# TensorE's order in a scan step: both rough score products ahead of the step's sums

## The chip, the cores and the metric

The kernel runs on one core of a Trainium2 chip. The metric is the device time of one launch in microseconds. The median of three runs of the kernel before is 12530.81 us (12523.07 to 12570.84). Engines are named as in the profile: PE is TensorE, DVE is VectorE, ACT is ScalarE, POOL is GpSimd, SP is SyncE, which issues most of the transfers.

## The reference

For each of 16 images of 192 channels and 32 x 32 positions, four layers run one after the other, each on the group-normalised input and added to it:

```
x = x + attention(gn(x))      # 6 heads of 32, softmax over 1024 positions
x = x + selective_scan(gn(x)) # 4 directions, 192 channels, 16 states, 1024 steps
x = x + top_k_mask(gn(x))     # depthwise conv, 30 largest of each channel kept
x = x + chunked_scan(gn(x))   # Mamba-2 block with 12 heads, chunks of 128
```

The second layer's recurrence, for every direction k, channel d and state n, is

```
h = h * exp(dt * A) + (dt * u) * b      # along 1024 positions
y = sum over n of h * c
```

Its dt is softplus of a projection with a bias. The first layer's softmax needs the largest score of each row, and the kernel takes it from a rough bf16 product.

## The kernel before

One loop runs over the images. In its first part two things are woven together: the **scan** of image b (second layer) and the **front** of image b+1, which is that image's attention, its norms and the set-up of its own scan (projections, dt and its softplus).

The scan has 96 steps (`NSTEP`), each with 128 rows (16 channels x 8 states) of 1024 positions. Step i is made of:
- POOL, L1234: the input dt*u*b of step i+3, into one of ten buffers;
- ACT, L1127 (`decay`): exp(dt*A) into the one PSUM tile `ps[2]`. The decay of step i+1 is written in step i and waits until scan i has read the tile;
- DVE, L1189: the scan itself. In every fourth step (`from_psum`, i % 4 == 1) the scan leaves its result in PSUM (L1179) and DVE multiplies by c itself (L1186); in the other steps POOL multiplies (L1250);
- PE, L1015 (`sums`): the sum over states of step i-2, four matmul records in the trace.

The front is written as 192 **half slots** (`HS`), two to a step. Each engine has a generator for it (`front_pe`, `front_act`, `front_dve`, `front_pool`, `front_sp`), and the scan's function of that engine calls `next(front)` twice in a step: on ACT, DVE and POOL once before and once after the step's own main instruction. So an item of an even half slot stands ahead of the step's decay (ACT) or scan (DVE), an item of an odd one behind it. Engines run their instructions in this written order; semaphores couple them. The tables at L516 to L525 give each item its half slot. Those that matter here:
- `PROJECT`, `VALUES` (steps 4 to 19, all in even half slots): the q, k and v projections, PE L675 and L687.
- `ROUGH` (half slots 17 to 112, one product in each): the rough product, PE L700, into the one PSUM bank `bank(3)`. In the next half slot DVE takes its row maximum (L917), and the next product waits for that.
- `UNIT`: 16 attention units for each of three pairs of heads. A unit is the scores (PE L725), their exp (ACT L869, one half slot later for the first two pairs, in the same one for the third) and, together with the next unit's scores, the sums of the weighted values (PE L737). I call the pairs 0, 1 and 2. Pair 0 has even half slots (52 to 82), pair 1 odd ones (87 to 117), pair 2 both.
- `MAX_ROWS`: the maxima turned into a row, PE L711, once DVE has joined them (L921), then copied by ACT (L832).
- `OUT_AT`: output projection (PE L749), added by DVE (L902) two half slots later; then the norm (`norm_*`), the transposed copy (ACT L880) and `LOWERED` (PE L760, ACT L885).
- `DT_AT`: six dt projections, PE L772 (`steps_of`). Two half slots later ACT adds the bias (L890), three later DVE clamps (L940), four later ACT takes the exp (L894).

On PE the step is written as

```
next(front)          # even half slot
if i >= 2:
    sums(i - 2)
next(front)          # odd half slot
```

Of the kernel before, what the change touches and what calls it, by code (L numbers as in the profile page):

```python
# [88 lines left out]
def build(nc, x, out, wqk, wv, wp, pb, xpw, dtw, dtb, alog, ds, lnw, lnb, cw, cb, wz, wx, wdt,  # L89
# [3 lines left out]
    with ctx:  # L93
# [424 lines left out]
        ROUGH = [17, 49, 81]  # L518
        MAX_ROWS = [49, 84, 119]
        UNIT = [[52 + 2 * k for k in range(16)], [87 + 2 * k for k in range(16)], [122 + 4 * k // 3 for k in range(16)]]  # L520

        EXP_LAG = (1, 1, 0)
        OUT_AT = (156, 158, 160, 162)
        LOWERED = (171, 172, 174, 175)
        DT_AT = (176, 178, 180, 182, 184, 186)  # L525

# [56 lines left out]
        def front_sp(sp, image):  # L583
            for hs in range(HS):
                t, m = sums_at(hs - 1)
                if t is not None:
                    sp.wait_ge(a_oc, 2 * t + m + 1)
                    for e in range(2):
                        rows, c = rows_of_head(2 * t + e)
                        sp.dma_start(OA[rows, c, HALF * m:HALF * m + HALF], OC[64 * e:64 * e + DH, :]).then_inc(a_u, 16)  # L590
                if hs == 165:
                    sp.wait_ge(a_x, 4)
                    for c, m in enumerate(CT):
                        sp.dma_start(x1_d[image, 128 * c:128 * c + m, :], XI[0:m, c, :]).then_inc(f_x, 16)
                if hs == 171:
                    sp.wait_ge(g_xn, 4)
                    for c, m in enumerate(CT):
                        sp.dma_start(xn_d[image, 128 * c:128 * c + m, :], XN[0:m, c, :]).then_inc(f_n, 16)
                for s in range(2):
                    if hs == 175 + 3 * s:  # L600
                        sp.wait_ge(m_xc, 2 * s + 2)
                        sp.dma_start(bc_d[image, s, :, :], XD[0:RP, s, :]).then_inc(m_bw, 16)
                yield
# [46 lines left out]
        def front_pool(pool):  # L650
            for hs in range(HS):
# [5 lines left out]
                if m == 1 and t >= 1:  # L657

                    c, n = t - 1, CT[t - 1]
                    pool.wait_ge(a_u, 64 * (t + 1))  # L660
                    pool.wait_ge(a_rl, 32 * (t + 1))
                    pool.tensor_tensor(OA[0:n, c, :], OA[0:n, c, :], RDB[0:n, c, :], ALU.mult).then_inc(a_o, 1)
                if hs == 169:
                    norm_pool(pool, 1)
                yield

        def front_pe(pe):
# [108 lines left out]
            for hs in range(HS):  # L776
# [18 lines left out]
                if hs in OUT_AT:  # L795
                    project_out(OUT_AT.index(hs) // 2, OUT_AT.index(hs) % 2)
                if hs == 167:
                    norm_pe(pe, 1)
# [7 lines left out]
        def front_act(act, stored):  # L806
            for hs in range(HS):
# [55 lines left out]
                if t is not None:  # L863
# [3 lines left out]
                    for e in range(2):  # L867
                        act.wait_ge(a_st, 2 * u + e + 1)
                        nc.scalar.activation(PT[:, 2 * (u % 2) + e, :], bank(e), ACT.Exp,  # L869
                                             scale=DH ** -0.5).then_inc(a_e, 1)  # L870
                if hs == 166:
                    norm_square(act, 1)
                if hs == 170:
                    norm_act(act, 1, (128, 128))
                if hs in (171, 172):

                    c = hs - 171
                    act.wait_ge(g_xn, 4)
# [18 lines left out]
        def front_dve(dve, image):  # L897
# [7 lines left out]
            for hs in range(HS):  # L905
# [20 lines left out]
                if hs - 2 in OUT_AT:  # L926
                    add(OUT_AT.index(hs - 2) // 2, OUT_AT.index(hs - 2) % 2)
                if hs == 161:
                    dve.wait_ge(a_x, 2)
                    norm_stats(0, XI)  # L930
                if hs == 165:
                    dve.wait_ge(a_x, 4)
                    norm_sums(dve, 1, XI, begun=True)
                if hs == 168:
                    norm_var(dve, 1)
# [71 lines left out]
        def scan_pe(pe, front):  # L1007
# [13 lines left out]
            for i in range(NSTEP):  # L1021
                next(front)
                if i >= 2:
                    sums(i - 2)
                next(front)

# [50 lines left out]
        def scan_sp(sp, b, front):  # L1077
            for i in range(NSTEP):
# [15 lines left out]
                if i % 2 == 0:  # L1094
# [3 lines left out]
                    if i + 2 * DTR < NSTEP:  # L1098
                        sp.wait_ge(m_da, i + 2)
                        spread_dt(sp, b, i + 2 * DTR, m_dtl[i // 2 % DTR])  # L1100
                if i == 93:

# [916 lines left out]
```

## Time and profile before

| | before |
|---|---|
| median of three runs | 12530.81 us |
| the profiled execution's own time | 12556.06 us |
| its span, first to last instruction | 12554.3 us |
| granted TensorE clock, mean | 0.839 |
| PE busy | 9985.9 us (80%) |
| DVE busy | 8321.4 us (66%) |
| POOL busy | 7736.3 us (62%) |
| ACT busy | 4365.6 us (35%) |
| L1186 on DVE, 384 times | mean 1225 ns |
| L869 on ACT, 1632 times | mean 591 ns |
| L921 on DVE, 51 times | mean 3649 ns |

Span and run time differ by under 2 us. No engine is busy all the time: the engines wait for each other in turn, and the engine with the largest share is not for that reason the bound. The granted clock is the share of TensorE's full 2.4 GHz that the chip gave; it is 1.0 or 0.5 at any moment, so 0.839 is a mix. Matmul records overlap in time, so their starts say more than their durations.

### The profile page before, as it was taken

The page shows a single profiled execution, that of the slowest core. Times are in us where ns is not written, and L with a number is a line of the kernel's source. Part 1 is how long each engine was busy: PE and PEld are TensorE (multiplying, and loading weights), DVE is VectorE, ACT ScalarE, POOL GpSimd, SP SyncE. Part 2 cuts the span into 40 slices and gives each one's busy share as a digit, 9 for nine tenths or more (in the row PEclk, how much of TensorE's full clock was granted, in tenths as well). Part 3 has the DMA queues.
Part 4 walks back from the last instruction along what each step waited for, and adds up shares of the span by engine and source line. Part 5 has one row for each costly group of instructions (what it writes and reads, how often), then busy time and mean ns, then how long its engine had stood idle before and what let it go on. Part 6 is the DMA issues. An engine that isn't in the chain of part 4 may idle for free. (4 is left out here: it accounts for less than half of the span.)

```text
span 12554.3 us, 91878 instructions
## 1 busy us (share of the span) xinstructions
PE 9985.9 (80%) x28440; PEld 2877.6 (23%) x28440; DVE 8321.4 (66%) x7943; ACT 4365.6 (35%) x5374; POOL 7736.3 (62%) x3710
## 2 busy tenths in 40 slices
PE   6787877878778787878878778787878878778787
PEld 1112222122222212122122222212122122222212
DVE  2367666667666667666667666667666767667666
ACT  1243333424334233333423334243333423334243
POOL 0384766837567474766847567484766847567583
PEclk9697878879788787888979788887878979788897
DMA  0352542524335242542524335152543524345252
GB/s 14 90 123 63 125 106 69 123 67 118 86 93 138 49 119 63 122 110 69 123 68 114 88 93 138 49 119 63 125 106 73 124 67 116 83 97 134 56 122 56
DMA packets 358663, 1181.05 MB, mean 94 GB/s; under 512 B 67483, under 2 KB 68747, under 8 KB 358023
## 3 DMA queue, kind: packets, MB, share of 16 engines
q1 hardware_dynamic: 331703, 1157.28, 37.0%
q10 hardware_dynamic: 24800, 15.62, 0.5%
q8 instruction: 259, 4.24, 0.1%
q14 instruction: 381, 3.12, 0.1%
q0 software_dynamic: 1520, 0.78, 0.0%
HBM read 1004.06 MB, written 156.02 MB: 92 GB/s over the span
## 5 line engine op out<-in xcount | busy, mean ns | idle before, releaser
L1234 POOL TENSOR_TENSOR arena<-arena 128x1024 f32<-128x1024 f32 x1536 | 3666.8, 2401 | 734.6 <-issue 712.3
L1250 POOL TENSOR_TENSOR arena<-arena 128x1024 f32<-128x1024 f32 x1152 | 2713.9, 2356 | 1414.1 <-DVE arena L1189 1411.7
L1015 PE MATMUL ps<-arena,sel_y 128*32 128x512 f32 x6144 | 3307.6, 673 | 231.2 <-POOL arena L1250 208.7
L1189 DVE TENSOR_TENSOR_SCAN arena<-ps,arena 128x1024 f32<-128x1024 f32 x1152 | 2630.2, 2283 | 773.4 <-ACT ps L1127 711.9
L1127 ACT ACTIVATE ps<-arena,v_na 128x1024 f32<-128x1024 f32 x1536 | 1716.3, 1117 | 3461.1 <-DVE arena L1189 2214.7
L917 DVE TENSOR_REDUCE arena<-ps 128x1 bf16<-128x512 f32 x1632 | 1115.0, 683 | 1259.2 <-PE ps L700 1259.2
L1015 PEld LDWEIGHTS ps<-arena,sel_y 128*32 128x32 f32 x6144 | 601.3, 118 | 2420.0 <-issue 2046.6
L869 ACT ACTIVATE arena<-ps 128x512 f32<-128x512 f32 x1632 | 879.7, 591 | 774.5 <-PE ps L725 774.1
L725 PE MATMUL ps<-arena 33*128 33x512 f32 x3264 | 988.2, 684 | 111.7 <-ACT arena L869 85.7
L1179 DVE TENSOR_TENSOR_SCAN ps<-ps,arena 128x1024 f32<-128x1024 f32 x384 | 878.0, 2286 | 297.0 <-ACT ps L1127 289.2
L700 PE MATMUL ps<-arena 32*128 32x512 bf16 x1632 | 678.6, 416 | 476.8 <-DVE arena L917 476.0
L737 PE MATMUL ps<-arena 128*64 128x512 f32 x3264 | 993.6, 691 | 0.0
L410 PE MATMUL ps<-g_mv,c_group 128*128 128x3 f32 (+1 forms) x528 | 128.1, 338 | 870.5 <-DVE g_mv L361 540.3
L417 POOL TENSOR_TENSOR g_t<-g_t,v_root 128x2 f32<-128x2 f32 x66 | 46.3, 702 | 973.1 <-DVE g_t L379 973.1
L700 PEld LDWEIGHTS ps<-arena 32*128 32x128 bf16 x1632 | 151.1, 93 | 1680.8 <-DVE arena L917 1076.6
L1186 DVE TENSOR_TENSOR arena<-ps,arena 128x1024 f32<-128x1024 f32 x384 | 470.4, 1225 | 45.8 <-DVE ps L1179 7.5
L1686 DVE SCALAR_TENSOR_TENSOR arena<-arena,v_mcw 128x1024 f32<-128x1024 f32 (+1 forms) x384 | 456.9, 1190 | 13.1
L1696 POOL TENSOR_SCALAR arena<-arena,v_mcw 128x640 f32<-128x640 f32 x144 | 164.2, 1143 | 463.6 <-ACT arena L1594 463.6
L1668 POOL TENSOR_TENSOR arena<-arena,c_heads 88x1536 bf16<-88x1536 bf16 x112 | 313.2, 2797 | 186.0 <-ACT arena L1622 176.9
L1858 POOL TENSOR_TENSOR arena<-arena 128x384 f32<-128x384 f32 x128 | 106.3, 830 | 482.3 <-DVE arena L1760 482.3
L725 PEld LDWEIGHTS ps<-arena 33*128 33x128 f32 x3264 | 258.8, 194 | 529.2 <-issue 273.0
L1594 ACT ACTIVATE arena<-ps 128x1024 f32<-128x1024 f32 x64 | 65.8, 1028 | 878.1 <-PE ps L1439 878.1
(217 smaller groups left out, 12005.8 us busy)
## 6 DMA issues: line engine op xcount, KB each, us to landing
arena<-scan_dtu SPq DMA_DIRECT2D x770, 512.0 KB, 6.1
arena<-scan_dt SPq DMA_DIRECT2D x770, 512.0 KB, 4.7
arena<-scan_bc SPq DMA_DIRECT2D x260, 512.0 KB, 6.9
scan_dt<-arena SPq DMA_DIRECT2D x68, 512.0 KB, 8.1
scan_dtu<-arena SPq DMA_DIRECT2D x68, 512.0 KB, 4.8
scan_dt<-arena SPq DMA_DIRECT2D x68, 256.0 KB, 4.1
scan_dtu<-arena SPq DMA_DIRECT2D x68, 256.0 KB, 4.7
XN<-arena SPq DMA_DIRECT2D x204, 64.0 KB, 4.3
```

The source lines that it names most:

```text
L700: nc.tensor.matmul(bank(3), QR[at:at + DH, t, Q * j:Q * j + Q], KR[at:at + DH, t, HALF * m:HALF * m + HALF], start=True, stop=True).then_i ...
L725: nc.tensor.matmul(bank(e), KK[r, t, Q * j:Q * j + Q], QQ[r, t, HALF * m:HALF * m + HALF], start=True, stop=True).then_inc(a_st, 1)
L737: mm = nc.tensor.matmul(bank(2)[64 * e:64 * e + 64, :], V[:, j, 2 * t + e, :], PT[:, 2 * (u % 2) + e, :], start=(j == 0), stop=(j == 7))
L869: nc.scalar.activation(PT[:, 2 * (u % 2) + e, :], bank(e), ACT.Exp, scale=DH ** -0.5).then_inc(a_e, 1)
L917: nc.vector.reduce_max(MXH[:, i // 2, i % 2:i % 2 + 1], bank(3), AX.X).then_inc(a_m, 1)
L1015: mm = nc.tensor.matmul(ps[3][32 * q:32 * q + 32, HALF * h:HALF * h + HALF], sel_y[:, r, :], step[:, i % NBUF, HALF * h:HALF * h + HALF], ...
L1127: nc.scalar.activation(ps[2][:], dtr[:, i // 2 % DTR, :], ACT.Exp, scale=v_na[:, at:at + 1]).then_inc(m_da, 1)
L1179: nc.vector.tensor_tensor_scan(ps[2][:, o], ps[2][:, o], step[:, i % NBUF, o], 0.0, ALU.mult, ALU.add).then_inc(m_h, 1)
L1186: nc.vector.tensor_tensor(step[:, i % NBUF, :], ps[2][:], Cb[2 * (k // 2) + f], ALU.mult).then_inc(m_hcv, 1)
L1189: nc.vector.tensor_tensor_scan(step[:, i % NBUF, o], ps[2][:, o], step[:, i % NBUF, o], 0.0, ALU.mult, ALU.add).then_inc(m_h, 1)
L1234: pool.tensor_tensor(step[:, i % NBUF, :], dur[:, i // 2 % DUR, :], Bb[2 * (k // 2) + f], ALU.mult).then_inc(m_bu, 1)
L1250: pool.tensor_tensor(step[:, i % NBUF, :], step[:, i % NBUF, :], Cb[2 * (k // 2) + f], ALU.mult).then_inc(m_hcp, 1)
```

## The change

On PE `sums(i - 2)` moves behind the second half slot. Every table entry from pair 1 on is raised by one half slot, and so are the fixed half slots of the norm, the copies and the transfers. The first `MAX_ROWS`, pair 0, `PROJECT`, `VALUES` and `ROUGH` keep theirs.

```diff
-        MAX_ROWS = [49, 84, 119]
-        UNIT = [[52 + 2 * k for k in range(16)], [87 + 2 * k for k in range(16)], [122 + 4 * k // 3 for k in range(16)]]
+        MAX_ROWS = [49, 85, 120]
+        UNIT = [[52 + 2 * k for k in range(16)], [88 + 2 * k for k in range(16)], [123 + 4 * k // 3 for k in range(16)]]
...
-        OUT_AT = (156, 158, 160, 162)
-        LOWERED = (171, 172, 174, 175)
-        DT_AT = (176, 178, 180, 182, 184, 186)
+        OUT_AT = (157, 159, 161, 163)
+        LOWERED = (172, 173, 175, 176)
+        DT_AT = (177, 179, 181, 183, 185, 187)
...
             for i in range(NSTEP):
                 next(front)
+                next(front)
                 if i >= 2:
                     sums(i - 2)
-                next(front)
```

The rest of the diff adds one to `hs == 165, 171, 175 + 3 * s` (SP), `169` (POOL), `167` (PE), `166, 170, 171, 172` (ACT), `161, 165, 168` (DVE), and turns SP's `i == 93` into `i == 94`. The order of SP's queue comes out the same.

PE in the steps with projections (about steps 9 to 15). L675 is a projection, L700 a rough product, L1015 the sums. Before:

```order
L700 MATMUL ps<-arena 128x512
L675 MATMUL ps<-XN,w_q 128x512 x2
L700 MATMUL ps<-arena 128x512
L1015 MATMUL ps<-arena,sel_y 32x512 x2
L700 MATMUL ps<-arena 128x512
```

After:

```order
L675 MATMUL ps<-XN,w_q 128x512 x2
L700 MATMUL ps<-arena 128x512 x2
L1015 MATMUL ps<-arena,sel_y 32x512 x2
L675 MATMUL ps<-XN,w_k 128x512 x2
L700 MATMUL ps<-arena 128x512 x2
```

The sums stood between the step's two rough products; now the two stand side by side, and sums and projection follow each other.

PE in the steps of pair 0 (steps 27 to 41). L725 are the scores, L737 the weighted values. Before:

```order
L700 MATMUL ps<-arena 128x512 x2
L725 MATMUL ps<-arena 128x512 x2
L737 MATMUL ps<-arena 64x512 x2
L1015 MATMUL ps<-arena,sel_y 32x512 x2
L700 MATMUL ps<-arena 128x512 x2
```

After:

```order
L700 MATMUL ps<-arena 128x512
L725 MATMUL ps<-arena 128x512 x2
L737 MATMUL ps<-arena 64x512 x2
L700 MATMUL ps<-arena 128x512
L1015 MATMUL ps<-arena,sel_y 32x512 x2
L700 MATMUL ps<-arena 128x512
```

The odd product stood behind unit and sums, right before the next even one. Now it stands between unit and sums.

ACT in the last steps (89 to 95). L1127 is the decay of the scan's next step, L890 the bias of a dt projection, L894 the exp of the one before. Before:

```order
L890 ACTIVATE arena<-ps,v_dtb 128x1024
L1127 ACTIVATE ps<-arena,v_na 128x1024
L894 ACTIVATE arena<-arena 128x1024
L890 ACTIVATE arena<-ps,v_dtb 128x1024
L1127 ACTIVATE ps<-arena,v_na 128x1024
L894 ACTIVATE arena<-arena 128x1024
L634 ACT_TABLE_LOAD
```

After:

```order
L890 ACTIVATE arena<-ps,v_dtb 128x1024
L1127 ACTIVATE ps<-arena,v_na 128x1024
L894 ACTIVATE arena<-arena 128x1024
L890 ACTIVATE arena<-ps,v_dtb 128x1024
L894 ACTIVATE arena<-arena 128x1024
L634 ACT_TABLE_LOAD
```

These are the last rows of the scan; the pattern of the first three repeats before them. All L890 and L894 have moved behind one decay more: the last decay stood behind the last L890, and now the last L890 stands behind the last decay. On DVE the clamps (L940) stay where they were, each right before a scan.

## Rows read from the trace of the kernel before

**Rows 1.** Waits: engine and line, waited for: us in total, times, longest us.
```profile
DVE arena L917 <- PE ps L700: 1259.2, 811, 24.2
```
**Rows 2.** Timeline, PE and DVE, one step of pair 0, third image: start, us, instruction [idle before <-releaser].
```profile
2239.41 2.28 DVE L1189 TENSOR_TENSOR_SCAN arena<-ps,arena 128x1024 f32<-128x1024 f32 x1
...
2239.56 0.39 PE L700 MATMUL ps<-arena 32*128 32x512 bf16 x1 [0.79 <-DVE arena L917]
...
2241.61 0.67 DVE L917 TENSOR_REDUCE arena<-ps 128x1 bf16<-128x512 f32 x1
...
2241.95 1.90 PE L1015 MATMUL ps<-arena,sel_y 128*32 128x512 f32 x4
...
2243.79 0.40 PE L700 MATMUL ps<-arena 32*128 32x512 bf16 x1
...
2244.22 0.69 DVE L917 TENSOR_REDUCE arena<-ps 128x1 bf16<-128x512 f32 x1 [1.94 <-PE ps L700]
...
2244.97 0.40 PE L700 MATMUL ps<-arena 32*128 32x512 bf16 x1 [0.79 <-DVE arena L917]
```
**Rows 3.** Windows, steps 26 to 41, 16 images: stretch, length, busy by engine, clock.
```profile
5921.96:6024.27 102.31, 88.22 (x219) 18.31 (x220) 63.64 (x55) 34.57 (x48) 67.00 (x29) 0.83 0.42 97
...
sum 1574.98, PE 1354.34 PEld 283.39 DVE 1018.41 ACT 552.52 POOL 1061.73; mean PE 84.65 PEld 17.71 DVE 63.65 ACT 34.53 POOL 66.36
```
**Rows 4.** The same over steps 43 to 56, pair 1; one image, and the sum.
```profile
759.58:825.23 65.65, 61.79 (x188) 14.10 (x187) 53.56 (x48) 32.78 (x45) 58.37 (x25) 1.00 0.65 153
...
sum 1050.04, PE 988.26 PEld 225.16 DVE 856.89 ACT 524.30 POOL 934.23; mean PE 61.77 PEld 14.07 DVE 53.56 ACT 32.77 POOL 58.39
```
**Rows 5.** Timeline, PE, one step with a projection, third image.
```profile
2082.12 0.39 PE L700 MATMUL ps<-arena 32*128 32x512 bf16 x1
...
2082.45 2.18 PE L675 MATMUL ps<-XN,w_k 128*128 128x512 f32 x4
...
2084.56 0.40 PE L700 MATMUL ps<-arena 32*128 32x512 bf16 x1
...
2084.88 1.90 PE L1015 MATMUL ps<-arena,sel_y 128*32 128x512 f32 x4
...
2086.72 0.40 PE L700 MATMUL ps<-arena 32*128 32x512 bf16 x1
```
**Rows 6.** Windows, steps 20 to 25 of the first image.
```profile
629.50:660.72 31.22, 23.91 (x55) 4.65 (x53) 25.12 (x22) 8.13 (x8) 27.79 (x13) 0.73 0.52 119
```
**Rows 7.** Windows over steps 9 to 19 of 16 images, the sum.
```profile
sum 897.78, PE 866.15 PEld 250.09 DVE 663.23 ACT 289.30 POOL 743.85; mean PE 54.13 PEld 15.63 DVE 41.45 ACT 18.08 POOL 46.49
```
**Rows 8.** Timeline, ACT and DVE, steps 90 to 95, third image.
```profile
2496.14 2.28 DVE L1189 TENSOR_TENSOR_SCAN arena<-ps,arena 128x1024 f32<-128x1024 f32 x1
...
2502.89 1.11 ACT L890 ACTIVATE arena<-ps,v_dtb 128x1024 f32<-128x1024 f32 x1 [0.22 <-PE ps L772]
...
2503.91 1.11 ACT L1127 ACTIVATE ps<-arena,v_na 128x1024 f32<-128x1024 f32 x1
...
2504.04 1.28 DVE L940 TENSOR_SCALAR arena<-ps,v_dtb 128x1024 f32<-128x1024 f32 x1 [0.26 <-ACT arena L890]
...
2505.24 2.28 DVE L1189 TENSOR_TENSOR_SCAN arena<-ps,arena 128x1024 f32<-128x1024 f32 x1
...
2512.70 1.12 ACT L1127 ACTIVATE ps<-arena,v_na 128x1024 f32<-128x1024 f32 x1 [1.20 <-DVE arena L1186]
...
2513.83 1.06 ACT L894 ACTIVATE arena<-arena 128x1024 f32<-128x1024 f32 x1
...
2513.92 2.29 DVE L1189 TENSOR_TENSOR_SCAN arena<-ps,arena 128x1024 f32<-128x1024 f32 x1
...
2514.79 1.10 ACT L890 ACTIVATE arena<-ps,v_dtb 128x1024 f32<-128x1024 f32 x1
...
2516.30 1.12 ACT L1127 ACTIVATE ps<-arena,v_na 128x1024 f32<-128x1024 f32 x1 [0.41 <-DVE arena L1189]
...
2517.52 2.29 DVE L1189 TENSOR_TENSOR_SCAN arena<-ps,arena 128x1024 f32<-128x1024 f32 x1
```

More of the change, by code:

```diff
@@ L590, in front_sp @@
                         sp.dma_start(OA[rows, c, HALF * m:HALF * m + HALF], OC[64 * e:64 * e + DH, :]).then_inc(a_u, 16)
-                if hs == 165:
+                if hs == 166:
                     sp.wait_ge(a_x, 4)
@@ L594, in front_sp @@
                         sp.dma_start(x1_d[image, 128 * c:128 * c + m, :], XI[0:m, c, :]).then_inc(f_x, 16)
-                if hs == 171:
+                if hs == 172:
                     sp.wait_ge(g_xn, 4)
@@ L599, in front_sp @@
                 for s in range(2):
-                    if hs == 175 + 3 * s:
+                    if hs == 176 + 3 * s:
                         sp.wait_ge(m_xc, 2 * s + 2)
@@ L662, in front_pool @@
                     pool.tensor_tensor(OA[0:n, c, :], OA[0:n, c, :], RDB[0:n, c, :], ALU.mult).then_inc(a_o, 1)
-                if hs == 169:
+                if hs == 170:
                     norm_pool(pool, 1)
@@ L796, in front_pe @@
                     project_out(OUT_AT.index(hs) // 2, OUT_AT.index(hs) % 2)
-                if hs == 167:
+                if hs == 168:
                     norm_pe(pe, 1)
@@ L870, in front_act @@
                                              scale=DH ** -0.5).then_inc(a_e, 1)
-                if hs == 166:
+                if hs == 167:
                     norm_square(act, 1)
-                if hs == 170:
+                if hs == 171:
                     norm_act(act, 1, (128, 128))
-                if hs in (171, 172):
-                    c = hs - 171
+                if hs in (172, 173):
+                    c = hs - 172
                     act.wait_ge(g_xn, 4)
@@ L927, in front_dve @@
                     add(OUT_AT.index(hs - 2) // 2, OUT_AT.index(hs - 2) % 2)
-                if hs == 161:
+                if hs == 162:
                     dve.wait_ge(a_x, 2)
                     norm_stats(0, XI)
-                if hs == 165:
+                if hs == 166:
                     dve.wait_ge(a_x, 4)
                     norm_sums(dve, 1, XI, begun=True)
-                if hs == 168:
+                if hs == 169:
                     norm_var(dve, 1)
@@ L1100, in scan_sp @@
                         spread_dt(sp, b, i + 2 * DTR, m_dtl[i // 2 % DTR])
-                if i == 93:
+                if i == 94:
                     sp.wait_ge(m_dtp, 6)
```

## The prediction

> **What bounds the kernel now.** I read the waits first, then the timeline of one step in each stage, then the same stage over all 16 images with the windows. The waits say that DVE idles 1259 us for the rough products [rows 1]: that is the wait the change is aimed at. The timeline shows how it arises in a step of pair 0 [rows 2]. PE starts an even product at 2239.56, then unit and sums (2241.95), and only then the odd product (2243.79): 4.23 us. DVE had finished the maximum it depends on at 2242.28 (2241.61 + 0.67) and then sits idle 1.94 us. From the odd product over its maximum (2244.22, 0.69 us) to the next even product (2244.97) it is 1.18 us, in which PE has 0.33 us of work. So a step lasts 5.41 us: PE's row of work, plus a wait of 0.85 us in which PE has nothing it may start.
>
> Over the 16 images the 16 steps of this stage take 1574.98 us, 98.4 an image or 6.15 a step [rows 3]. That is 0.74 us a step more than 5.41. The granted clock there lies below 1, down to 0.83 in the image shown, so part of the time TensorE runs at 1.2 GHz and not at 2.4. In the stage of pair 1, where the unit stands between the odd and the even product, the same work takes 1050.04 us over 16 images and 14 steps: 4.69 a step, at a clock of 1.00 [rows 4].
>
> In the steps with projections [rows 5] the same happens as with pair 1: even product to odd 2.16 us (sums between them), odd to even 2.44 us (projection between them). Both gaps are longer than the 1.18 us of the maximum, which is thereby hidden.
>
> **The change, part by part (for one image, times 16 at the end).**
>
> *Pair 0, steps 26 to 41.* The order becomes even product, unit, odd product, sums. Even to odd is 2.39 us of PE work (2239.56 to 2241.95), odd to even 0.33 + 1.84 = 2.17; both exceed 1.18, so a step is 4.56 us, PE's own work. DVE's round is shorter: scan to maximum 2.20, maximum 0.67, next product after 0.06, its result after 0.43, maximum to scan 0.61, together 3.97. DVE's own product, 1.2 us in every fourth step (L1186 in the profile's table), lifts that step to about 5.2. This is the pattern of pair 1, so I take its measured 4.69 a step, 75.0 us for 16 steps against 98.4: -23.4. The bounds of what is left of the half clock are 0 (as with pair 1) and 11.8 (16 x 0.74, all of it). I take 3, since the stage before this one runs at a lowered clock, 0.73 in the image shown [rows 6]: **-20.4 us**.
>
> *Projections and values, steps 9 to 19.* Here the change undoes what the order had. It becomes projection, even product, odd product, sums. Even to odd is now the naked 1.18, then 0.33 + 1.84 for odd product and sums, then projection and even product at 2.10: 5.45 us a step. DVE does not bound it, not even in its long step (0.43 + 0.61 + 2.20 + 1.2 = 4.4 after the odd product, and the even product's result is there after 4.7). The stage has 11 steps, 60.0 us, against 897.78 / 16 = 56.1 [rows 7]: +3.9. To that comes the clock. PE was busy 54.1 of 56.1 us here; now 0.85 us of each 5.45 are a wait with nothing to do, as in pair 0 before, 0.85 of 5.41. There it cost 0.74 us a step [rows 2, 3]. The bounds are 0 and 11 x 0.74 = 8.1; I take 6.5, because the two rounds are nearly alike: **+10.4 us**.
>
> *Weighed against the Trainium skill.* "TensorE: Matmul & The Clock Gate" (HAM oscillation, and the table at its end) says that TensorE stays warm as long as there are no long idle gaps between bursts of matmuls. The rows of pair 0 speak against it: no gap there is longer than 1.2 us, and the clock is still 0.83. By that rule the clock would add nothing to the projections; this is the first rival below.
>
> *The first row of maxima, step 24.* It stays in half slot 49, and the sums now wait behind it and behind DVE's long L921. Before step 25's first product PE then has 1.84 us of sums left, at half clock 3.7. DVE's own scan and product cover part of it. Bounds 0 and 2.6, I take **+1.3**. Between 20 and 26, where PE has only products and sums, the DVE round of 3.97 rules as before: 0.
>
> *The biases and clamps of dt, steps 90 to 95.* This is the price that the change's table hides. ACT's L890 stood ahead of the decay and ran while DVE scanned; the decay started at the end of the scan or just behind it (2502.89 and 2503.91), and the clamp (2504.04) ran on DVE beside the decay. From scan to scan this was 3.74 us. Moved by one half slot, exp and bias stand behind the decay, which waits for the scan, while DVE still wants the clamp before its next scan. So everything follows in one file: scan to decay 2.38 (2513.92 to 2516.30), decay to exp 1.13 (2512.70 to 2513.83), exp to bias 0.96, bias to clamp 1.15 (2502.89 to 2504.04), clamp to scan 1.20: 6.82 us [rows 8]. From scan 90 to scan 95 there are five such rounds and one such product, 35.3 us, against 2517.52 - 2496.14 = 21.4: +13.9. The first bias, before scan 90, waits for PE today as well; there it can cost 0 to 1.1 (its own duration), I take 0.6: **+14.5 us**. Nothing covers this: PE, POOL and DVE all wait for the next scan, and the set-up behind the scan (its logarithms) starts later by as much.
>
> *What costs nothing.* The exps of pairs 1 and 2 move behind the decay. For pair 1 the scan ends 3.24 us after the odd product (0.43 + 0.61 + 2.20); decay (1.1) and two exps (0.6 each) end at 5.5, and the next scores start only at 2.17 + 0.33 in the next step, at 7.1. For pair 2, PE's row of three units and two sums in two steps stays the same, and the decay has over a microsecond of room. DVE's additions of the output projection move behind the scan; they no longer hold up scan 79, but what ends this stage is PE's row of projections and sums up to the group's end, which is the same, so I count 0, with 0 to -4 as bounds. The norm's steps land in the shadow of a decay. POOL's order and SP's are practically the same.
>
> Sum: -20.4 + 10.4 + 1.3 + 14.5 = **+5.8 us an image, +93 us in all**. The profiled execution's own time is 12556.06; it becomes 12649. It lies 25 us above the median of the runs, and against that median I predict **12624 us**. A difference under 0.5%, 63 us, can't be told from none here; that is 3.9 us an image.
>
> **The rivals.**
>
> *The clock stays full in the projections* (the skill's rule). Then that term is +3.9, the sum -0.7 an image: 12520 us, no change. For it: in these stages the clock was 1 so far. Against it: the idle share will be the one of pair 0. 0.22.
>
> *The clamps do not close the round*, the faster side. The mechanism: if ACT could finish exp and bias before the scan wants its clamp, the last steps would keep 3.74 us. Its place is ACT's queue from step 89 on, its price the 13.9; it decides when a round stays under about 5 us. Then it is -8.1 an image, 12401 us, 1% faster. Against it stands the order itself: L890 is behind L1127, and L1127 waits for the scan. 0.08.
>
> *Pair 0 keeps its half clock* (DVE's own product in every fourth step leaves PE idle about 0.7 us, and a low clock carried over from step 25 may persist). Then pair 0 gives -11.6 only, the sum is +14.6, 12765 us. Against it: pair 1 has the same idle time and never lost its clock. 0.12.
>
> *The change does not do what it says*: the step of pair 0 stays at 5.41, because ACT's exp behind the decay holds the next scores. The sum would be +26, 12950 us. Against it: by the count above the exp ends 1.6 us before the scores need it. 0.03.
>
> **How the numbers follow.** The forecast has 0.55, pair 0's half clock 0.12, the change that fails 0.03: mostly slower. The full clock (0.22) is no change but for little on either side, the open round 0.08 is faster. Of the forecast's own 0.55 I count 0.47 as slower and 0.08 as no change, since its terms together move by 4 us an image. Slower 0.64, same 0.26, faster 0.10. The range takes in the full clock at its lower end and half of the way to pair 0's half clock at its upper: 12510 to 12740.
>
> **What would show it.** Steps of pair 0 at 4.6 us with a clock near 1, and DVE's wait for L700 there gone. Steps 9 to 19 at 5.45 and more, with DVE waiting for L700 and a clock under 1. From 90 to 95 about 6.8 us from scan to scan, with DVE's L940 waiting for ACT's L890. The prediction is wrong if the last steps keep 3.74 us, or if pair 0 gains under 15 us an image.

## The result and the profile after

| | before | changed |
|---|---|---|
| median | 12534.56 us (12523.07 to 12570.84) | 12748.86 us (12724.75 to 12776.83) |
| profiled execution, its own time | 12556.06 us | 12776.83 us |
| its span | 12554.3 us | 12775.0 us |
| granted clock, mean | 0.839 | 0.833 |
| PE busy | 9985.9 us | 10041.8 us |
| L921 on DVE, 51 times, mean | 3649 ns | 4492 ns |

The changed kernel is slower: the ratio is 1.0164, with a 95% interval of 1.0143 to 1.0185. The forecast was 12624 us and its range ended at 12740, so the direction was right and the size was not. It missed by 125 us of 12749.

Spans from decay to decay by stage give the bill. Every number is the mean over 16 images, in us; the stages outside the scan are taken from decay 95 to the next image's decay 0 (15 of them), and "forecast" is the term on record.

| stage | before | changed | difference | forecast |
|---|---|---|---|---|
| steps 0 to 8 | 41.3 | 41.1 | -0.2 | 0 |
| 9 to 19, projections and values | 56.1 | 67.3 | +11.2 | +10.4 |
| 20 to 25, first row of maxima | 31.3 | 33.1 | +1.8 | +1.3 |
| 26 to 41, pair 0 | 98.4 | 85.3 | -13.1 | -20.4 |
| 43 to 56, pair 1 | 65.6 | 67.7 | +2.1 | 0 |
| 62 to 73 | 58.3 | 57.3 | -1.0 | 0 |
| 78 to 89, output projection | 63.5 | 59.3 | -4.2 | 0 (0 to -4) |
| 90 to 94, and outside the scan | 20.9 and 268.8 | 34.1 and 272.5 | +13.2 and +3.7 | +14.5 |

Steps 42, 57 to 61 and 74 to 77 are left out; they differ by -0.1, +0.3 and 0.0. Over the whole span the changed kernel is 220.7 us longer, 13.8 an image, where the forecast had 5.8.

Here are the windows of the changed kernel (columns as in [rows 3]): steps 9 to 19, 26 to 41, 43 to 56 and 90 to 94, each with one image and the sum of 16. They answer to [rows 7], [rows 3] and [rows 4].

```profile
5156.19:5223.04 66.85, 58.96 (x122) 15.57 (x121) 42.39 (x35) 18.41 (x22) 46.72 (x20) 0.87 0.40 94
...
sum 1077.53, PE 951.32 PEld 247.30 DVE 678.28 ACT 295.07 POOL 747.45; mean PE 59.46 PEld 15.46 DVE 42.39 ACT 18.44 POOL 46.72
...
5256.70:5342.54 85.84, 76.13 (x222) 16.86 (x221) 68.64 (x55) 34.54 (x49) 66.09 (x29) 0.96 0.53 124
...
sum 1364.70, PE 1220.94 PEld 270.06 DVE 1084.33 ACT 552.90 POOL 1061.49; mean PE 76.31 PEld 16.88 DVE 67.77 ACT 34.56 POOL 66.34
...
5346.74:5414.37 67.63, 61.87 (x202) 14.46 (x201) 53.84 (x48) 30.95 (x43) 58.38 (x25) 1.00 0.63 148
...
sum 1083.24, PE 990.75 PEld 230.65 DVE 860.94 ACT 494.94 POOL 934.28; mean PE 61.92 PEld 14.42 DVE 53.81 ACT 30.93 POOL 58.39
...
5573.23:5607.14 33.91, 27.09 (x52) 6.41 (x50) 18.63 (x11) 14.53 (x15) 14.88 (x7) 0.85 0.16 45
...
sum 544.85, PE 455.42 PEld 110.26 DVE 298.14 ACT 232.87 POOL 222.69; mean PE 28.46 PEld 6.89 DVE 18.63 ACT 14.55 POOL 13.92
```

In pair 0 two things differ. PE's busy time fell from 84.65 to 76.31 us an image [rows 3]: that is the clock coming back (0.96 in the image shown, 0.95 over the 16, where the kernel before has 0.87). But DVE's busy time rose from 63.65 to 67.77, although its work is the same 55 instructions in the image shown. Something on DVE got longer. In the projections PE is busy 59.46 us instead of 54.13 [rows 7], at a clock of 0.87: the half clock has moved there.

The last steps behave as the prediction drew them. ACT and DVE, third image, answering to [rows 8]: decay, exp and bias stand in a file behind the scan, then the clamp, and from scan to scan it is 2532.76 - 2526.06 = 6.70 us.

```profile
2526.06 2.28 DVE L1189 TENSOR_TENSOR_SCAN arena<-ps,arena 128x1024 f32<-128x1024 f32 x1
...
2528.43 1.12 ACT L1127 ACTIVATE ps<-arena,v_na 128x1024 f32<-128x1024 f32 x1 [3.61 <-DVE arena L1189]
2529.49 1.04 ACT L894 ACTIVATE arena<-arena 128x1024 f32<-128x1024 f32 x1
2530.44 1.09 ACT L890 ACTIVATE arena<-ps,v_dtb 128x1024 f32<-128x1024 f32 x1
...
2531.56 1.28 DVE L940 TENSOR_SCALAR arena<-ps,v_dtb 128x1024 f32<-128x1024 f32 x1 [3.22 <-ACT arena L890]
2532.76 2.28 DVE L1189 TENSOR_TENSOR_SCAN arena<-ps,arena 128x1024 f32<-128x1024 f32 x1
```

Step by step, pair 0 divides cleanly. Most steps have the 4.56 us that the count of PE's work gave (3.98 where there is less on PE, 5.89 with DVE's own product). Two kinds stand out. Steps 34 and 50 take 7.00 and 6.99 us, where they took 5.45 and 4.57. And step 41 takes 10.58 us on average, where it took 7.37. These are DVE's rows of step 34, third image:

```profile
2236.74 0.68 DVE L917 TENSOR_REDUCE arena<-ps 128x1 bf16<-128x512 f32 x1
2239.75 1.28 DVE L1164 SCALAR_TENSOR_TENSOR arena<-arena,v_dsum,ps 128x1024 f32<-128x1024 f32 x1 [2.33 <-PE ps L1015]
2240.95 0.69 DVE L917 TENSOR_REDUCE arena<-ps 128x1 bf16<-128x512 f32 x1
```

L1164 is `taken`, which adds a finished group's sums to the output. On DVE it stands behind the maximum of the even product (2236.74) and ahead of the maximum of the odd one (2240.95), and it waits for the sums of two steps earlier. Those sums now come behind the odd product. So DVE idles 2.33 us, while the odd product's result lies ready behind `taken`, and the next even product waits for its maximum. And these are DVE's and POOL's rows of step 41, third image:

```profile
2272.45 0.67 DVE L917 TENSOR_REDUCE arena<-ps 128x1 bf16<-128x512 f32 x1
2273.15 6.70 DVE L921 TENSOR_TENSOR arena<-arena 128x16 bf16<-128x16 bf16 x1
2279.78 0.68 DVE L917 TENSOR_REDUCE arena<-ps 128x1 bf16<-128x512 f32 x1
...
2270.47 2.37 POOL L1234 TENSOR_TENSOR arena<-arena 128x1024 f32<-128x1024 f32 x1
2272.79 2.37 POOL L1250 TENSOR_TENSOR arena<-arena 128x1024 f32<-128x1024 f32 x1
2275.10 4.72 POOL L1234 TENSOR_TENSOR arena<-arena 128x1024 f32<-128x1024 f32 x2
```

L921 is the maximum of the two halves' row maxima, 16 numbers a lane. It starts while POOL works, and ends at 2279.85, when POOL's third operation in a row ends (2275.10 + 4.72 = 2279.82). In the same step of the kernel before it was held for only one of POOL's operations:

```profile
2253.14 1.91 DVE L921 TENSOR_TENSOR arena<-arena 128x16 bf16<-128x16 bf16 x1
...
2252.66 2.35 POOL L1250 TENSOR_TENSOR arena<-arena 128x1024 f32<-128x1024 f32 x1 [0.80 <-DVE arena L1189]
2254.98 4.74 POOL L1234 TENSOR_TENSOR arena<-arena 128x1024 f32<-128x1024 f32 x2
```

Mean durations of L921 over 16 images are 2.82, 1.91 and 6.87 us in steps 25, 41 and 57 of the kernel before, and 1.91, 5.83 and 6.55 in the changed one. The long form was in the trace of before: in step 57 of every image, and in step 25 of four of them (7.27 to 7.65 us), but never in step 41.

### The profile page after: what moved, and what is told of

It reads as the page before. It is cut to its first block and busy times, and to the rows that moved or that the text cites. A ratio compares the mean times of both kernels' runs of the same rounds, so it can differ in the third digit from the quotient of the medians.

```text
span 12775.0 us, 91878 instructions
## 1 busy us (share of the span) xinstructions
PE 10041.8 (79%) x28440; PEld 2912.4 (23%) x28440; DVE 8380.2 (66%) x7943; ACT 4357.3 (34%) x5374; POOL 7723.9 (60%) x3710
## 5 line engine op out<-in xcount | busy, mean ns | idle before, releaser
L1250 POOL TENSOR_TENSOR arena<-arena 128x1024 f32<-128x1024 f32 x1152 | 2717.4, 2359 | 1624.6 <-DVE arena L1189 1623.1
L1015 PE MATMUL ps<-arena,sel_y 128*32 128x512 f32 x6144 | 3340.5, 690 | 177.5 <-POOL arena L1250 155.0
L1127 ACT ACTIVATE ps<-arena,v_na 128x1024 f32<-128x1024 f32 x1536 | 1717.1, 1118 | 4145.6 <-DVE arena L1189 2604.3
L700 PE MATMUL ps<-arena 32*128 32x512 bf16 x1632 | 683.0, 419 | 528.1 <-DVE arena L917 528.0
L1015 PEld LDWEIGHTS ps<-arena,sel_y 128*32 128x32 f32 x6144 | 607.4, 119 | 2136.3 <-issue 1829.6
L725 PE MATMUL ps<-arena 33*128 33x512 f32 x3264 | 992.9, 687 | 119.0 <-ACT arena L869 114.4
L737 PE MATMUL ps<-arena 128*64 128x512 f32 x3264 | 958.8, 668 | 0.0
L700 PEld LDWEIGHTS ps<-arena 32*128 32x128 bf16 x1632 | 151.1, 93 | 1775.7 <-DVE arena L917 1040.7
L1686 DVE SCALAR_TENSOR_TENSOR arena<-arena,v_mcw 128x1024 f32<-128x1024 f32 (+1 forms) x384 | 456.9, 1190 | 13.1
L725 PEld LDWEIGHTS ps<-arena 33*128 33x128 f32 x3264 | 259.9, 195 | 541.3 <-ACT arena L869 264.0
L940 DVE TENSOR_SCALAR arena<-ps,v_dtb 128x1024 f32<-128x1024 f32 x102 | 131.0, 1284 | 347.7 <-ACT arena L890 347.7
```

The source lines that it names most:

```text
L700: nc.tensor.matmul(bank(3), QR[at:at + DH, t, Q * j:Q * j + Q], KR[at:at + DH, t, HALF * m:HALF * m + HALF], start=True, stop=True).then_i ...
L725: nc.tensor.matmul(bank(e), KK[r, t, Q * j:Q * j + Q], QQ[r, t, HALF * m:HALF * m + HALF], start=True, stop=True).then_inc(a_st, 1)
L737: mm = nc.tensor.matmul(bank(2)[64 * e:64 * e + 64, :], V[:, j, 2 * t + e, :], PT[:, 2 * (u % 2) + e, :], start=(j == 0), stop=(j == 7))
L1015: mm = nc.tensor.matmul(ps[3][32 * q:32 * q + 32, HALF * h:HALF * h + HALF], sel_y[:, r, :], step[:, i % NBUF, HALF * h:HALF * h + HALF], ...
L1127: nc.scalar.activation(ps[2][:], dtr[:, i // 2 % DTR, :], ACT.Exp, scale=v_na[:, at:at + 1]).then_inc(m_da, 1)
L1250: pool.tensor_tensor(step[:, i % NBUF, :], step[:, i % NBUF, :], Cb[2 * (k // 2) + f], ALU.mult).then_inc(m_hcp, 1)
```

## The experiments

All times are medians, and all ratios are to the kernel before on the same chip, with 95% intervals. Four kernels came first: one for each of the two losses, one for the gain alone, one for the wait in front of `taken`.

**The dt units put back.**

```
-        DT_AT = (177, 179, 181, 183, 185, 187)
+        DT_AT = (176, 178, 180, 182, 184, 186)
```

> After with the six dt entries alone back at 176 to 186, so that bias and exp stand ahead of the decay again. Theory (clamp chain): steps 90 to 94 fall from 34.1 to about 21 us, and the scan's end comes another 3 us earlier behind the last decay; 16 us an image, 250 us in all, 12495 us. Rival (the end of the scan is held by something else, or the loss returns behind the scan): under 100 us gained.

Measured: 12501.37 us, ratio 0.9951 (0.9933 to 0.9969). Steps 90 to 94 are back at 20.2 us an image and the stretch outside the scan at 268.8. The ratio lies 0.0213 under the changed kernel's, 267 us or 16.7 an image. The file of ACT and DVE is the loss of the last steps, and it is the largest one.

**The old order in the projections alone** (the changed kernel).

```
             for i in range(NSTEP):
+                late = i < 8 or i >= 20
                 next(front)
+                if i >= 2 and not late:
+                    sums(i - 2)
                 next(front)
-                if i >= 2:
+                if i >= 2 and late:
                     sums(i - 2)
```

> After with the sums between the two products again in steps 8 to 19, the projections and values. Theory (both products side by side leave TensorE idle for one maximum a step): steps 9 to 19 fall from 67.3 to 56.1 us at a clock of 1, steps 20 to 25 by 1 or 2 us; 12 us an image, 195 us in all, 12555 us. Rival (the loss of this stage is the half clock and not the order): the steps stay at 5.5 us or more.

Measured: 12545.19 us, ratio 0.9993 (0.9977 to 1.0009). Steps 9 to 19 take 56.4 us an image at a clock of 0.98. Confirmed: the order of the sums is the loss of the projections, with 0.0171 of the ratio.

**The late sums in pair 0 alone** (the kernel before; the same edit, with `late = 26 <= i < 42`).

> Before with the sums behind the second half slot in steps 26 to 41 only, all tables as before. Theory (this is the change's one gain, and it is the order there alone): steps 26 to 41 take 85 us as in after against 98, clock about 0.96, all other stages as before; 13 us an image, 205 us in all, 12330 us. Rival (the gain needs the shifted tables, or is given back in pair 1, as part of it seemed to be in after): 12450 us or more.

Measured: 12415.81 us, ratio 0.9891 (0.9866 to 0.9916). That is a gain of 1.1%, and neither theory's number. Steps 26 to 41 take 86.8 us an image, against 98.4: -11.6, not -20. The gain is thus smaller than the sum had it even where the table of half slots is untouched and nothing else changed. L921 in step 41 lasts 5.53 us here as well, and step 34 takes 7.00. Steps 43 to 56 give back 1.9 us (65.6 to 67.5), all of it in step 43, where the order changes back (5.50 to 7.37).

**`taken` behind the first maximum of the step after**, that of the odd product (the changed kernel).

```
                 next(front)
+                for g_ in range(3):
+                    if i == GROUP_END[g_] + 3:
+                        taken(g_)
                 dve.wait_ge(m_bu, i + 1)
...
                 next(front)
-                for g_ in range(3):
-                    if i == GROUP_END[g_] + 2:
-                        taken(g_)
```

> After with DVE's group result (L1164 and L1169, which wait for the sums of step i-2) moved one place later, behind the maximum of the odd product. Theory (the group result now holds up the odd maximum, because its sums stand behind the odd product on TensorE): the steps behind 33 and 49, 7.0 us in after, fall to about 5, with a clock mended around 35, so 3 to 6 us an image and about 70 us in all: 12680 us. Rival (pair 0 misses its gain through L921 and the clock alone): no change, 12749 us.

Measured: 12763.88 us, ratio 1.0161 (1.0134 to 1.0188): no gain, the expectation was wrong. Step 34 fell only to 6.40 us, as the wait was halved and not gone:

```profile
L1164 DVE SCALAR_TENSOR_TENSOR arena<-arena,v_dsum,ps x32: 1271/1276/1282, 711.4 to 12267.3; 128x1024 f32<-128x1024 f32 x16, 64x1024 f32<-64x1024 f32 x16
its engine sat idle before it (us, times) until:
  PE ps L1015: 36.5, 32
```

That is 36.5 / 32 = 1.14 us each, where the changed kernel has 74.4 / 32 = 2.33. And what steps 26 to 41 won (85.3 to 82.3, of which 0.9 in step 41, where L921 was long in fewer images), steps 43 to 56 lost in part (67.7 to 69.8): steps 52 and 53 took 6.64 and 6.92 us. So this run did not decide whether the wait costs anything.

**L921 with one input.** The next four are this edit in three kernels, and both losses undone. This one goes after the second suspect.

```
-  nc.vector.tensor_tensor(MX[:, two], MXH[:, two, 0], MXH[:, two, 1], ALU.max).then_inc(a_mx, 1)
+  nc.vector.reduce_max(MX[:, two], MXH[:, two, :], AX.X).then_inc(a_mx, 1)
```

In the changed kernel:

> Edit: the changed kernel, and the maximum of the two halves' row maxima (L921, a tensor_tensor with two SBUF inputs) is a reduce_max over one SBUF input instead. In the changed kernel L921 lasted 5.8 us on average in step 41 and 6.6 us in step 57, from before GpSimd's second operation of the step to the end of its third, where the same instruction took 0.26 us in a step 25 in which GpSimd stood idle at its start. Theory A (the two-input form is held off by GpSimd's back-to-back operations): the single-input form takes under 1 us everywhere, step 41 falls from 10.6 to about 6.0 us, step 57 from 11.0 to about 6.5 us, 9 us per image, so about 12610 us, 1 per cent under the changed kernel. Theory B (it waits for something else, so that the form does not matter, or GpSimd's own chain of three operations sets the end of the step anyway): within 0.3 per cent of the changed kernel, 12750 us.

Measured: 12560.2 us, ratio 1.0014 (0.9996 to 1.0032), 0.0150 under the changed kernel's, more than the 9 us an image that I expected (0.0150 x 12540 / 16 = 11.8). L921 in this kernel:

```profile
L921 DVE TENSOR_REDUCE arena<-arena x51: 185/186/188, 155.5 to 12087.8; 128x16 bf16<-128x32 bf16 x51
```

The durations are minimum, median and maximum in ns; in the changed kernel they are 175, 6680 and 6877. POOL's three operations still run back to back beside it. Step 41 takes 5.89 us instead of 10.58, step 57 takes 4.94 instead of 10.71. This form isn't held off. The stall had cost clock as well: PE idled 4.5 us in step 41 in 13 of the 16 images, and the clock of step 42 was 0.64, where it is 1.00 here.

In the kernel before:

> Edit: the kernel before, with the same single-input maximum at L921. There it lasted 2.8 us in step 25, 1.9 us in step 41 and 6.9 us in step 57. Theory A: step 57 falls by some 4.5 us, steps 25 and 41 by up to 1 us each, 5 to 6 us per image, about 12460 us against 12550; and the changed kernel with the same edit gains 4 us per image more than this one, which is the part of the lost gain of pair 0 that the stall took. Theory B: no change, 12550 us, in both.

Measured: 12438.57 us, ratio 0.9898 (0.9864 to 0.9932). By the spans the edit takes 6.9 us an image off the kernel before and 14.6 off the changed one, 7.7 more, where I had expected 4 more. The two kernels with the mended L921 can be compared without the stall in either. Their windows of steps 26 to 41, first the kernel before with this edit, then the changed one:

```profile
sum 1597.68, PE 1372.57 PEld 286.20 DVE 990.70 ACT 552.55 POOL 1078.56; mean PE 85.79 PEld 17.89 DVE 61.92 ACT 34.53 POOL 67.41
```

```profile
sum 1288.55, PE 1204.27 PEld 267.34 DVE 995.30 ACT 553.96 POOL 1061.82; mean PE 75.27 PEld 16.71 DVE 62.21 ACT 34.62 POOL 66.36
```

(1597.68 - 1288.55) / 16 = 19.3 us an image. The term on record was 20.4, but against the kernel before as it stands, 98.4 and not the 99.9 of this pair; from there to 80.5 it is 17.9. Over all stages the difference between the two spans is 12542.0 - 12444.0 = 98 us, and the sum on record was 93.

**Both losses undone**, the dt units and the order in the projections.

> Edit: the changed kernel with both of its losses undone: the dt units back at half slots 176 to 186, and the sums ahead of the even half slot's product in steps 0 to 19. Each alone gave back 1.7 to 2.1 per cent (13 to 16 us per image). If the two are apart in the program and the terms add: 12290 us, 2.1 per cent under the kernel before, with scan steps 9 to 20 at 56 us and 90 to 95 at 20 us per image. Rival: the two shift the state in which TensorE's clock enters the later steps, and one gives back part of the other: 12350 us or more.

Measured: 12257.67 us, ratio 0.9764 (0.973 to 0.9798). 1.0164 - 0.0213 - 0.0171 = 0.978: the two add, within the interval.

**The same with the one-input L921.**

> Edit: the previous one (dt units and projections as in the kernel before) with the single-input maximum at L921. Theory A: 9 us per image under it, about 12150 us, 3.2 per cent under the kernel before. Theory B: as the previous one, 12290 us.

Measured: 12117.86 us, ratio 0.9651 (0.9618 to 0.9683). Steps 26 to 41 take 80.2 us and 57 to 61 take 21.0 where they took 27.1.

**`taken` behind the scan** (the kernel just told). The edit is the one of the first move, but the three lines stand between the scan and the second `next(front)` of step `GROUP_END + 3`.

> Edit: the kernel of the run before this one (dt units and projections as before, single-input maximum), and the addition of a finished group to the output (taken) is made one step later, between the scan and the odd maximum of that step, instead of ahead of the even maximum. In steps 34 and 50 VectorE idled 2.3 us before it, because TensorE makes the sums that it waits for only behind the odd product, and the two steps took 7.0 us. Theory: VectorE has its scan to do while those sums are made, and only the 1.3 us of the addition itself stay on its path: steps 34 and 50 fall from 7.0 to 5.9 us, 3 us per image with the third group, so about 12070 us against 12120. Rival: the even product of the next step is held up by the sums behind the addition, as with the first move (steps 52 and 53 then took 6.6 and 6.9 us), and the time is within 0.3 per cent of 12120 us.

Measured: 12036.95 us, ratio 0.9611 (0.959 to 0.9633). The ratio lies 0.0040 under that of the kernel without it, 50 us, as the theory had it, but the two intervals overlap; the medians, from two chips, are 81 us apart. The stages are the firmer evidence. `taken` (now L1167) has no wait of DVE before it at all, and it runs while PE is at its own work:

```profile
2137.12 0.69 DVE L917 TENSOR_REDUCE arena<-ps 128x1 bf16<-128x512 f32 x1 [0.49 <-PE ps L700]
2137.72 2.28 DVE L1192 TENSOR_TENSOR_SCAN arena<-ps,arena 128x1024 f32<-128x1024 f32 x1
2139.92 1.26 DVE L1167 SCALAR_TENSOR_TENSOR arena<-arena,v_dsum,ps 128x1024 f32<-128x1024 f32 x1
```

Step 34 takes 3.98 us and step 35 5.15. Steps 26 to 41 gain 3.5 us an image (80.2 to 76.7) and steps 43 to 56 gain 2.7 (67.7 to 65.0, which is the kernel before's 65.6 and a little less). The two profiled spans are 85 us apart. So the wait of `taken` was a real part of the loss, and the first move put it in a place where it was still early. This kernel beats both: 3.9% under the kernel before.

**Two filler matmuls in the projections** (the changed kernel with the one-input L921).

```
                 if t is not None:
                     rough(t, r)
+                if hs in PROJECT and hs >= 16:
+                    pe.wait_ge(a_qkc, PROJECT.index(hs) - 1)
+                    keep_clock(2, bank((PROJECT.index(hs) + 1) % 3))
+                if hs in VALUES:
+                    v = VALUES.index(hs)
+                    pe.wait_ge(*((a_qkc, 11 + v) if v < 2 else (a_vc, v - 1)))
+                    keep_clock(2, bank((v + 1) % 3))
```

> Edit: the changed kernel with the single-input maximum, and two 512-column matmuls on zeros behind the even half slot's product in each half slot with a projection or values, into the bank that the next projection overwrites. They add 0.86 us of TensorE work at full clock, most of it in the 0.8 us in which TensorE waits there for the even maximum. In the changed kernel each of the steps 11 to 19 shows two durations, 1.6 us apart (5.2 and 6.8 us in step 12), the longer one where the granted clock was half. Theory A (of the 10 us that the projections lose 3.8 us are the order and the rest is the half clock): the clock of steps 9 to 20 rises to 0.97 or more and the stage falls from 66 to 60 to 62 us per image, about 12490 us against 12560. Theory B (it is the order alone, and the clock costs nothing; then the fillers are only in the way): 68 us or more in the stage, 12600 us or more.

Measured: 12414.85 us, ratio 0.9912 (0.9884 to 0.9941), 1% under the same kernel without fillers. Its steps 9 to 19, one image and the sum:

```profile
5028.23:5089.06 60.83, 58.30 (x149) 16.16 (x149) 42.40 (x35) 18.08 (x22) 46.32 (x20) 1.00 0.40 99
...
sum 972.60, PE 932.14 PEld 257.84 DVE 678.39 ACT 289.31 POOL 742.79; mean PE 58.26 PEld 16.11 DVE 42.40 ACT 18.08 POOL 46.42
```

The clock is 1.00, and the stage takes 972.60 / 16 = 60.8 us where it took 66.1, with more matmuls in it. What is left over the kernel before's 56.1 is the order and the fillers' own work. Steps 20 to 25 gain 2.6 us too; step 20 alone falls from 7.07 to 5.43.

**The sums early again in pair 1** (the kernel with both losses undone and the one-input L921; `late = i < 8 or 20 <= i < 42 or i >= 58`).

> Edit: the kernel with dt units and projections as before and the single-input maximum, with the sums also ahead of the even product in steps 42 to 57 (pair 1), where TensorE's clock was full in both kernels. Theory: the late sums gain nothing there and cost the wait before taken in step 50: the stage of steps 43 to 57 falls from 67.7 to 65.6 us per image, about 12085 us against 12120. Rival: with the single-input maximum the clock of pair 1 is no longer held in the old order (it is the sums' place that holds it), and the stage takes 70 us or more, 12150 us or more.

Measured: 12367.09 us, ratio 0.9869 (0.9849 to 0.9889), 2.2% more than without it. The theory was wrong by far. Steps 43 to 56:

```profile
5179.59:5263.74 84.15, 72.39 (x202) 15.59 (x200) 53.64 (x48) 30.79 (x43) 58.33 (x25) 0.87 0.52 124
...
sum 1357.31, PE 1169.05 PEld 250.65 DVE 858.33 ACT 492.64 POOL 934.04; mean PE 73.07 PEld 15.67 DVE 53.65 ACT 30.79 POOL 58.38
```

**The table alone, with the old order everywhere** (the changed kernel with its three lines of `scan_pe` as before).

> Edit: the changed kernel with the sums back ahead of the even half slot's product in all steps: the table of half slots alone is changed (units on first half slots, dt units one later), not TensorE's order. Theory: the table gives the loss of the dt units (16 us per image with the step behind the scan) and the 4 us that steps 78 to 90 gained, and leaves pair 0's steps with their half clock (98 us per image in steps 26 to 42) and the projections at 56 us: 12530 + 16 x 12 = about 12720 us. Rival: moving the units to first half slots is enough to bring pair 0's clock up, so that the swap only costs: steps 26 to 42 at 90 us or less, 12600 us or less.

Measured: 12894.9 us, ratio 1.0303 (1.0285 to 1.0322), another miss of mine. Steps 26 to 41 stay at 100.8 us, as the theory had it, but steps 43 to 56 go from 65.6 to 82.6. PE's rows of pair 1 in this kernel, third image:

```profile
2326.53 3.00 PE L1015 MATMUL ps<-arena,sel_y 128*32 128x512 f32 x4
2329.46 0.40 PE L700 MATMUL ps<-arena 32*128 32x512 bf16 x1
2330.65 0.40 PE L700 MATMUL ps<-arena 32*128 32x512 bf16 x1 [0.79 <-DVE arena L917]
2330.97 1.13 PE L725 MATMUL ps<-arena 33*128 33x512 f32 x4
```

Unit and sums between even and odd product, then the odd and the next even product with nothing between them but a wait of 0.79: this is pair 0 of the kernel before [rows 2]. The table moves the units of pairs 1 and 2 from second to first half slots, into the place where the early sums already are. Both misses have this one cause, and I could have read it from the table. So in pair 1 the two parts of the change belong together (the new order everywhere over the old table was not run): over that table the swap is worth 1.0303 - 1.0164 = 0.0139 in all (15.5 us an image in steps 26 to 41 and 14.9 in 43 to 56, less the 10.8 it costs in 9 to 19, 4.4 in 20 to 25, 5.4 in 57 to 61 and 6.7 in 78 to 89), and the table without it loses 3%. Most of the 5.4 is L921 once more: it has its two-input form in this kernel, but never took longer than 1.92 us, not in step 57 either (6.07 us a step, 10.71 in the changed kernel).

## Why the prediction was right and wrong

**Projections and values, +10.4: right, and for its reasons.** Measured +11.2. The order alone was put at 3.9 and the clock at 6.5. Among the kernels with the one-input L921 the stage goes from 56.5 (kernel before) to 66.1 (changed), and with fillers to 60.8: 4.3 for the order, what the fillers cost included, and 5.3 for the clock. The steps show it singly too: step 12 has one of two lengths, the short one in 12 images and the long one in 4, and these are one of each, from the changed kernel's windows:

```profile
592.02:597.17 5.15, 4.36 (x11) 1.04 (x10) 3.58 (x3) 1.72 (x3) 4.41 (x3) 1.00 0.19 42
1352.15:1358.97 6.82, 6.03 (x10) 1.20 (x10) 3.58 (x3) 1.81 (x3) 4.42 (x3) 0.75 0.01 1
```

A step at full clock is 5.15, and one in which the half clock falls on PE's chain of products and projection is 6.82. The first rival, full clock in the projections, has fallen, and with it what the Trainium skill would make of this stage ("TensorE: Matmul & The Clock Gate", HAM oscillation and the table at its end, warm as long as no long gap lies between bursts). No gap of PE there is longer than 0.79 us and the clock of the stage is 0.87. The trace does not agree with that rule. What the prediction said of pair 0, that no gap there is longer than 1.2 us, was not exact: of 261 gaps of over half a microsecond 240 are of 0.8 us, and 21 of 1.6 to 1.9.

**Pair 0, -20.4: the step that failed.** Measured -13.1. The order did what was said. Most steps are at 4.56 and the clock is at 0.95. But 13.1 is under the 15 that the prediction gave as the mark of its being wrong. What failed is the sentence "so I take its measured 4.69 a step, 75.0 us for 16 steps". The rows it rests on are steps 43 to 56 [rows 4]. They leave out step 57, the one in which pair 1 has its L921, at 6.87 us, while pair 0's 16 steps hold the corresponding step 41. The 16 steps from 42 to 57 took 80.9 us in the kernel before; with them, and the same 3 for the clock, the term would have been -14.5.

In the changed kernel two steps stand above the pattern. Step 41 takes 10.58 us where it takes 5.89 without the stall, 4.7 more: this is L921. Step 34 takes 7.00 where step 50, its counterpart in pair 1, took 4.57 in the kernel before, 2.4 more: this is the wait of `taken`. Together they are 7.1 of the 7.3 that are missing. The 3 for the half clock were about right. With both mended (`taken` behind the scan) the stage takes 76.7 us, at a clock of 0.99.

I had L921's mean of 3649 ns in the table of the profile and spoke of "DVE's long L921" for step 24's row, but did not read its durations step by step. They were 1.91 us in step 41 and 6.87 in step 57, so its length is not that of its own work and can change in either direction.

**Pair 1, 0: wrong by 2.1, the second step that failed.** "What costs nothing" did not list `taken`. It waits for the very sums that the change moves, and DVE has a maximum queued behind it. DVE's idle time before it was 12.4 us in 16 of the 32 executions of L1164 in the kernel before, and 74.4 us in all 32 in the changed one. The third group's `taken`, L1169, went from 22.7 to 55.5 us in 16 executions, 2.05 an image, which is what step 82 rose by. Moving it behind the scan gave back 2.7 us in pair 1 and 3.5 in pair 0. A moved step has those who wait for it, and I had looked only at the sums' place on PE.

**dt's biases and clamps, +14.5: right in kind, and 2 short.** Putting them back gave 16.7 us an image. The rounds are 6.70 us (8.04 with DVE's product) where 6.82 was forecast. The windows end at decay 95, so the last exp, bias and clamp show in the +3.7 of the stretch outside the scan. The second rival (the round stays open) is out.

**Row of maxima, +1.3:** measured +1.8 in steps 20 to 25, and 3.3 with the one-input L921 in both kernels. **Output projection, 0 with -4 as bound:** -4.2, at the bound. Steps 79, 85 and 88 fell (8.07 to 3.60, 7.71 to 4.94, 5.88 to 3.60 us), 81 and 82 rose (5.35 to 8.34, 5.50 to 7.55).

**Pair 0 keeps its half clock** (third rival): its 12765 us is nearest to the measured time, but it is not what happened. The clock came back to 0.96, and what was missing of the gain went to a DVE instruction and to a wait of DVE's. The time alone would have confirmed the wrong rival. That it was so near is luck. **The change that does not do what it says** is out, too: 4.56 us a step.

The sum of the forecast was 5.8 us an image. Measured are 13.8, and 6.1 (98 us) where L921 is mended in both kernels: the stall was by far the largest missing term. That the rest comes so near the forecast is in part luck. Between the two mended kernels pair 0 gains 1.1 less than its term, the row of maxima costs 2.0 more, pair 1 1.7 more, the last steps with the stretch outside the scan 3.1 more. Against that the output projection gains 4.2, steps 62 to 73 gain 1.5, and the projections and step 42 cost 0.8 less each.

Why the stall catches step 41 in the new timing (13 of 16 images at 6.7 us) and escaped in the old one is settled in part. In both kernels L921 starts while POOL runs L1250, and more of POOL's work follows at once. But in the kernel before POOL had idled for 0.80 to 2.43 us just before that L1250 in all 16 images, and in the changed one in none. In the eight kernels with the two-input form L921 began within one of POOL's operations 384 times. Where POOL had been idle before that operation, 75 times, L921 was never held beyond its end. Where POOL had run without a break, 309 times, it was held for over 4 us in 186. What lets it in early in the others, 3 of the 16 in step 41, stays open.

## What to carry over

When a stage is priced by the pattern of another, its window has to hold the same instructions, the closing step with its odd ones included; and an instruction whose durations spread forty-fold in one trace (174 to 7648 ns for 16 numbers a lane) should be understood before anything near it is moved. Of a step that moves on one engine, list those that wait for its result, and for each what is queued behind it: here `taken` held up a maximum. A table of half slots and an order of calls can be two halves of one move: the table alone was worse here than both or none, while the order alone in pair 0, where the table keeps its units, was better than both.

## What the runs showed of the hardware

**A two-input operation on DVE is held off by POOL.** The tensor_tensor of L921, both inputs in SBUF, took 0.17 to 0.18 us each of the 24 times that POOL was not at work at its start, and 6.9 us where POOL ran three operations back to back. All 384 that began within an operation of POOL ended 0.03 to 0.07 us behind the end of one of its operations; the row of step 41 above begins 0.36 us into the first of the three and ends 0.03 us after the last. The same maximum as a reduce of one input took 0.19 us each of 51 times, in the same place. That one edit was worth 1.0% in the kernel before and 1.5% in the changed one. This fits the lock that the Trainium skill tells of ("SBUF — State Buffer", SBUF: two separate sides, and Who interferes with whom): DVE and GpSimd share a pair of ports, a DVE operation with two SBUF inputs contends for it with a GpSimd operation that reads SBUF, and whoever holds it blocks the other for the whole instruction. The traces agree with the blocking, and go further: DVE was kept out for three instructions, not one. That the ports are the cause is the skill's account; the runs show that the form of the instruction decides, but no run changed the number of inputs alone, since the edit changes the operation too.

**TensorE's clock fell where gaps of 0.8 us came in every step.** In steps in which PE's row repeats a wait of 0.79 us with no work to put in it, the clock went between its two levels, 1.2 and 2.4 GHz: 0.87 in the projections of the changed kernel, 0.87 and 0.88 in pair 1 in the two kernels that have the new table and the sums early. Two matmuls on zeros in the wait left no gap over 0.26 us and brought it to 1.00, and the stage from 66.1 to 60.8 us. Here work that filled a wait paid although it computes nothing.
